# A reordered prefix of an attention and mixture-of-experts block: GpSimd's roots and splits, ScalarE's norms, the first row maxima

## The reference

```
x = x + layernorm(attn(layernorm(x)))
x = x + layernorm(experts(layernorm(x)))
```

```
qq, kq  = Q @ Wc2q + bc2q, K @ Wc2q + bc2q
fid     = (qq . kq) / max(|qq| |kq|, 1e-8)
qw      = fid * (1 + 0.1 sin(pi fid))
probs   = softmax(0.5 qw + 0.5 Q K^T / sqrt(HD))
```

## Time and profile before

| | us |
|---|---|
| median of 3 runs | 478.31 (477.62 to 478.55) |
| the profiled execution | 475.81 |
| its span | 474.1 |

### The profile page before, as it was taken

The page is one execution under the profiler, slowest core; times in us unless marked ns, Lnnn a source line. Parts: engine busy times, 40 slices in busy tenths (PEclk is TensorE's granted clock), DMA queues, the critical chain, the costliest instruction groups (busy, mean ns, idle before and its releaser), DMA issues.

```text
span 474.1 us, 9099 instructions
## 1 busy us (share of the span) xinstructions
PE 369.6 (78%) x2782; PEld 264.2 (56%) x2782; DVE 366.3 (77%) x895; ACT 321.9 (68%) x612; POOL 236.3 (50%) x340
## 2 busy tenths in 40 slices
PE   0976579999999999998998799756010999999950
PEld 0755336666666666665665433635000799999950
DVE  5587798999999999999985533699898148777771
ACT  1347448999999999999877554847510677776620
POOL 7458436555555555555310204000647728887773
PEclk9998858999999999999887999996655799999995
DMA  9606543676666777767719992000103959887400
GB/s 208 23 0 168 125 99 92 149 180 178 170 171 164 169 171 169 170 142 187 164 47 145 148 150 35 1 0 2 42 29 112 271 180 258 242 237 206 108 21 2
DMA packets 87084, 60.87 MB, mean 128 GB/s; under 512 B 16189, under 2 KB 79681, under 8 KB 87030
## 3 DMA queue, kind: packets, MB, share of 16 engines
q1 hardware_dynamic: 79814, 54.69, 52.3%
q0 software_dynamic: 2496, 4.29, 2.6%
q10 hardware_dynamic: 4720, 1.25, 1.3%
HBM read 35.90 MB, written 25.21 MB: 129 GB/s over the span
## 4 chain that ended last, share of the span: by engine, by line
DVE 45%; PE 28%; issue 9%; POOL 8%; ACT 6%; DMA 2%; POOLq 0%; DVEq 0%; SPq 0%; ACTq 0%
DVE big L1841 13%; DVE mxs L1818 11%; DVE big L1871 5%; POOL out_dram L848 5%; PE ps L1623 5%; PE ps L1635 5%; PE ps L1426 3%; PE ps L1211 2%; ACT big L965 2%; PE ps L1525 2%; PE ps L1520 2%; POOL fst L841 1%; DVE gb L1689 1%; DVE u_sb L1880 1%; DVE u_sb L2000 1%
## 5 line engine op out<-in xcount | busy, mean ns | idle before, releaser
L1841 DVE SCALAR_TENSOR_TENSOR big<-big,ps 128x1024 f32<-128x1024 f32 x64 | 74.1, 1215 | 4.2 <-ACT big L955 4.1
L1818 DVE TENSOR_REDUCE mxs<-ps 128x4 f32<-128x1024 f32 x64 | 74.0, 1218 | 1.6 <-PE ps L1248 0.9
L955 ACT ACTIVATE big<-ps 128x1024 f32<-128x1024 f32 x64 | 62.5, 1028 | 7.5 <-PE ps L1391 7.2
L834 POOL DMA_INDIRECT sorted_rows<-proj,sl_i x32 | 33.1, 1036 | 51.4 <-issue 43.6
L848 POOL DMA_INDIRECT out_dram<-arena,fidx x46 | 46.5, 1012 | 15.3 <-issue 9.7
L1623 PE MATMUL ps<-arena,big 128*128 128x256 f32 x184 | 45.3, 390 | 0.6 <-ACT arena L1153 0.6
L1635 PE MATMUL ps<-big,arena 128*128 128x128 f32 x368 | 44.8, 275 | 0.0
L1248 PE MATMUL ps<-arena 96*128 96x256 bf16 x256 | 39.4, 284 | 4.9 <-DVE mxs L1818 2.7
L1635 PEld LDWEIGHTS ps<-big,arena 128*128 128x128 f32 x368 | 42.9, 192 | 0.3 <-ACT arena L1162 0.3
L1871 DVE TENSOR_TENSOR big<-big,ps 128x1024 f32<-128x1024 f32 x32 | 37.9, 1217 | 5.2 <-PE ps L1413 5.1
L753 POOL CAST mtok<-mxs 128x16 bf16<-128x16 f32 x16 | 3.2, 198 | 74.8 <-DVE mxs L1818 74.8
(11 more groups left out here) (347 smaller groups left out, 854.4 us busy)
## 6 DMA issues: line engine op xcount, KB each, us to landing
big<-in_L_ffn_w_dram SPq DMA_DIRECT2D x42, 256.0 KB, 3.3
qk_parts<-proj SPq DMA_DIRECT2D x16, 384.0 KB, 3.2
arena<-qk_parts SPq DMA_DIRECT2D x32, 192.0 KB, 3.5
sorted_rows<-zrow SPq DMA_DIRECT2D x16, 266.0 KB, 5.9
arena<-qk_parts SPq DMA_DIRECT2D x32, 128.0 KB, 4.0
x_all<-sorted_rows SPq DMA_DIRECT2D x23, 133.0 KB, 3.2
sorted_rows<-zrow SPq DMA_DIRECT2D x2, 1263.5 KB, 23.6
sorted_rows<-zrow SPq DMA_DIRECT2D x2, 1197.0 KB, 20.1
```

Source lines behind the costliest of these rows:

```text
L955: nc.scalar.activation(W[par][:, n, :], src, ACT.Sin, scale=PI * (1 - 1e-6)).then_inc(sin_ready, 1)
L1818: nc.vector.tensor_reduce(mxs[:, b1 % 2, :, 2 * n:2 * n + 2], src, AX_X, ALU.max, negate=True).then_inc(unit_free, 1)
L1841: nc.vector.scalar_tensor_tensor(W[par][:, n, :], W[par][:, n, :], 10.0, f, ALU.add, ALU.mult).then_inc(unit_free, 1)
```

## The change

`by_scalar` becomes (2, 4, 5, 6, 7): the norms of groups 5 and 7 move from VectorE to ScalarE, behind the squares of groups 1 and 4. GpSimd takes the root of group 6 ahead of the split of q and k of batch 0, and splits u of batch 0 ahead of q and k of batch 1. All four max units of batch 0 are made before the flag's matmuls or right behind them, three of them ahead of the branch on VectorE; the reciprocals of the second part come between the maxima of batch 1. SyncE's transfers are sorted anew.

```
--- before.py
+++ after.py
@@ -385,7 +385,7 @@
                 return gb[:, 1, :, :].rearrange("p t n -> p (t n)")
             return projf[:, NT * ROW + g * GT * P:NT * ROW + (g + 1) * GT * P]
 
-        by_scalar = (2, 4, 6)
+        by_scalar = (2, 4, 5, 6, 7)
 
 
         SUMS = [("t", 0), ("x", 0), ("t", 1), ("x", 1), ("t", 2), ("t", 3), ("x", 2), ("x", 3)]
@@ -557,15 +557,15 @@
             put_qk(0)
             get_qk(0)
             put_qk(1)
+            put_u(0)
             get_qk(1)
-            put_u(0)
+            get_u(0)
             put_u(1)
-            get_u(0)
             put_qk(2)
+            put_max(0)
             get_u(1)
+            get_max(0)
             get_qk(2)
-            put_max(0)
-            get_max(0)
 
             def body(b, par, first, last, slow):
                 if not last:
@@ -732,12 +732,12 @@
             pool_rstd(4)
             pool_rstd(5)
             ones_under(2)
+            pool_rstd(6)
             split_qk(0)
-            pool_rstd(6)
             pool_rstd(7)
-            split_qk(1)
             root_out(0)
             split_u(0)
+            split_qk(1)
             split_u(1)
             split_qk(2)
             pool.wait_ge(post_loaded, 16 * 17)
@@ -930,10 +930,14 @@
             for g in range(NG):
                 if g + 2 < NG:
                     turn_x(g + 2)
-                if g + 4 < NG and g + 4 in by_scalar:
+                if g in (0, 2):
                     x_norm(g + 4)
                 take_v(g)
                 squares(g)
+                if g == 1:
+                    x_norm(5)
+                if g == 4:
+                    x_norm(7)
                 if g == 2:
                     roots(0)
                     take_qk(2, ps[:, 0, :])
@@ -1336,13 +1340,15 @@
                     turn_u(1)
             pe.wait_ge(qk_out, 3)
             max_unit(0, 0)
+            pe.wait_ge(v_out, NG - 1)
+            max_unit(0, 1)
+            pe.wait_ge(v_out, NG)
+            max_unit(0, 2)
             pe.wait_ge(flag_all, 1)
             for i in range(2):
                 mm = nc.tensor.matmul(ps[0:1, 7, i * P:(i + 1) * P], small[:, 4 + i:5 + i], ident[:, :], start=True, stop=True)
             mm.then_inc(flag_all, 1)
-            pe.wait_ge(v_out, NG)
-            max_unit(0, 1)
-            max_unit(0, 2)
+            max_unit(0, 3)
 
             def body(b, par, first, last, slow):
                 i3 = b % 3
@@ -1439,7 +1445,6 @@
                     mm.then_inc(h_tr, 1)
 
                 if first:
-                    max_unit(0, 3)
                     max_unit(1, 0)
                     turn_max(0)
                     for n in range(1, HP):
@@ -1763,6 +1768,13 @@
                 nc.vector.tensor_scalar(wo_c[:, :], wo_sb[:, :], mean_w[:, 0:1], None, ALU.subtract)
                 nc.vector.tensor_scalar(be2c_bc[:, :], be2_bc, mean_w[:, 1:2], None, ALU.subtract)
 
+            def top(b1, n):
+                dve.wait_ge(unit_ready, unit_no["max", b1, n] + 1)
+                if b1 >= 2:
+                    dve.wait_ge(m_split, 2 * (b1 - 1))
+                src = slot_of("max", b1, n).rearrange("p (h t k) -> p t h k", h=2, t=TPB)
+                nc.vector.tensor_reduce(mxs[:, b1 % 2, :, 2 * n:2 * n + 2], src, AX_X, ALU.max, negate=True).then_inc(unit_free, 1)
+
             ln_stats(0)
             ln_stats(1)
             x_norm(0)
@@ -1804,28 +1816,21 @@
                     clamp(0)
                 if g == 3:
                     reciprocals(0)
+            top(0, 0)
             norm_out(NG - 1)
             root_in(1)
             dve.wait_ge(flag_mins, 2)
             nc.vector.tensor_tensor(small[:, 4:6], small[:, 0:2], small[:, 2:4], ALU.min).then_inc(flag_all, 1)
             clamp(1)
 
-            def top(b1, n):
-                dve.wait_ge(unit_ready, unit_no["max", b1, n] + 1)
-                if b1 >= 2:
-                    dve.wait_ge(m_split, 2 * (b1 - 1))
-                src = slot_of("max", b1, n).rearrange("p (h t k) -> p t h k", h=2, t=TPB)
-                nc.vector.tensor_reduce(mxs[:, b1 % 2, :, 2 * n:2 * n + 2], src, AX_X, ALU.max, negate=True).then_inc(unit_free, 1)
-
-
-            top(0, 0)
+            top(0, 1)
             dve.wait_ge(flag_all, 2)
             nc.vector.tensor_reduce(small[0:1, 6:8], ps[0:1, 7, 0:2 * P].rearrange("p (a n) -> p a n", a=2), AX_X, ALU.min).then_inc(flag_all, 1)
             dve.wait_ge(flag_all, 3)
             nc.vector.tensor_tensor(small[0:1, 0:1], small[0:1, 6:7], small[0:1, 7:8], ALU.mult).then_inc(flag_all, 1)
             dve.wait_ge(flag_all, 4)
             nc.vector.tensor_scalar(flag[0:1, :], small[0:1, 0:1], 1.001 * EPS_COS ** 2, None, ALU.is_lt).then_inc(flag_ready, 1)
-            top(0, 1)
+            top(0, 2)
             before_batches = own_steps[0]
 
             def body(b, par, first, last, slow):
@@ -1881,11 +1886,11 @@
                                             ALU.mult).then_inc(h_done, 1)
 
                 if first:
-                    top(0, 2)
                     top(0, 3)
-                    for n in range(HP):
+                    top(1, 0)
+                    reciprocals(1)
+                    for n in range(1, HP):
                         top(1, n)
-                    reciprocals(1)
                 if slow:
                     norms()
                 if first:
```

25 lines of the change are left out of this document (12 added, 13 removed).

## The result

| | before | after |
|---|---|---|
| median of 7 runs beside each other, us | 477.62 (476.46 to 478.55) | 479.17 (478.71 to 481.62) |
| the profiled execution, us | 475.81 | 478.71 |
| its span, us | 474.1 | 477.0 |

The ratio is 1.0043 with an interval of 1.0023 to 1.0062: by it the changed kernel is about 2 us slower (the two medians differ by 1.55). The forecast was 477.9 and no change, in a range of 476.3 to 479.6. The time lies in the range, but its sign is that of rival 1, the falling clock.

What follows compares the result with a forecast made beforehand. The prediction took batch 0's head as the bound: `make_uv(7)`'s end, then VectorE's path to the third weight. A loss of 0.3, weights 1.2 earlier and a 0.8 stall left -0.4: 477.9 us, range 476.3 to 479.6.

Steps and rivals of the forecast that it cites:

- rival 1: Clock falls in the idle ahead of `make_uv(7)`, which takes 3.48 instead of 1.95: 478.7 to 479.5 us; chance 0.27.
- Norms and root of the early groups: Projections of the prefix: `make_uv(4)` starts at 35.6 instead of 38.55, `make_uv(6)` ends near 45.9, 2.6 us ahead of before.
- The gain is lost at `turn_u(1)`: GpSimd's list holds `turn_u(1)` until 48.6; `make_uv(7)` behind it ends at 50.85 at 2.4 GHz, a loss of 0.3.
- VectorE from `make_uv(7)` on: VectorE's maxima and reciprocals up to batch 0's weights: these could start at 67.0, 1.2 earlier; the branch's 0.77 wait stays.
- the sum: The forecast's total: -0.4 on the profiled execution, 475.81 to 475.4, so a median of 477.9; chance 0.41.
- What is late next: Batch 0's third weight, wanted at 69.3, waits 0.8 for its sine, out at 70.1; the gain left is 0.4.
- The fourth weight: Batch 0's last weight moves from 71.66 to some 72.0, under the transposes and matmuls of unit 0 (3.7 us).
- SyncE at nothing: Batch 1's reads, issued from 50.0 to 52.8 instead of from 44.94, still land before its first max unit: priced at nothing.
- Rival 2: Clock comes back earlier in batch 0, before the transposes: 1.5 us less for transposes and matmuls, 476.4; chance 0.12.
- Rival 3: GpSimd gains when VectorE's norms leave: `turn_u(1)` up to 1.4 earlier, 476.5 us; chance 0.06.
- Rivals 4 and 5: Weights' stall absent, 477.1 us, chance 0.08; or batch 1's reads arrive late, 479.5 us and more, chance 0.06.
- Rival 4: No stall at batch 0's weights, through q and k at 2.4 GHz or a quicker sine: 0.8 more gain, 477.1; chance 0.08.

Runs made afterwards that it cites:

- e12: The kernel before, unchanged, run once more as a kernel of its own: 477.96 us, ratio 0.9999.
- e1: The changed kernel with six matmuls whose output nobody reads, put ahead of `turn_u(1)`: 476.58 us, ratio 0.9990.
- e4: The changed kernel with the old order of maxima, reciprocals and max units: 479.05 us, ratio 1.0051.
- e8: The changed kernel with the reciprocals back behind all four maxima of batch 1: 476.72 us, ratio 1.0008.
- e2: The changed kernel with `turn_u(1)` behind `make_uv(7)` in TensorE's list: 475.96 us, ratio 0.9975.
- e3: The kernel before with only the new order of maxima, max units and reciprocals: 477.40 us, ratio 0.9995.
- e5: e2 with ScalarE's copy of q and k of batch 3 ahead of the third sine, in batch 0 only: 474.97 us, ratio 0.9966.
- e7: e2 with `split_qk(1)` and `get_qk(1)` in their old places and both `turn_u` behind `make_uv(7)`: 474.72 us, ratio 0.9963.
- e11: The changed kernel, unchanged, run once more for a second trace: 479.62 us, ratio 1.0040.
- e6: e2 with fifteen matmuls that nobody reads in four of TensorE's waits: 471.13 us, ratio 0.9887.
- e9: e7 with e5's copy and sixteen filling matmuls, none behind cos unit 2: 474.38 us, ratio 0.9942.
- e10: The kernel before with ten unread matmuls, six ahead of the flag's and four ahead of the branch: 475.49 us, ratio 0.9969.

## Why the prediction was wrong

**Norms and root of the early groups: right.** `make_uv(4)` started at 35.64 (forecast 35.6), at 2.4 GHz (1.97 instead of 3.48). ScalarE normed group 6 from 33.38 (33.4), the copies behind the roots began at 38.12 (38.2), and `make_uv(6)` ended at 45.44 (45.9).

**The gain is lost at `turn_u(1)`: right in place, wrong in price.** GpSimd's `split_u(1)` ended at 48.41 (48.6), and `make_uv(7)` started at 48.70. The failed step is "ends at 50.85 if the clock is 2.4 GHz: a loss of 0.3". It ended at 52.33: a loss of 1.8. This term was priced at the high clock on the strength of one row, the idle of 2.63 ahead of 35.90 at a clock of 1.00. That was a weak precedent. In the same trace the clock fell at 38.2, inside the next idle (of 1.99, up to 38.55), when TensorE had done 0.66 of work since the first one (granted 0.98 from 38.0 to 38.2, 0.50 from 38.2 to 38.4). In e12, the same kernel, it fell at 37.1, also inside that second idle. The idle of the changed kernel was also longer than forecast, 3.02 instead of 2.7; whether 2.7 would have kept the clock no run shows. Rival 1 named this mechanism, its place and a price of at most 1.55; measured were 0.97, 1.31, 1.37 and 1.68 (`make_uv(7)` of 2.92, 3.26, 3.32 and 3.63, less 1.95). It also said that a quarter of `make_uv(7)` at the low clock decides; in the first trace nearly all of it was. It got a chance of 0.27; the clock fell in all four traces with this idle. e1 only fills the idle, and the slowdown goes; e4 has the idle without the new tail, and the slowdown stays. So the step and its place are shown. The one trace that stands across is e8, which has the idle and a `make_uv(7)` of 2.92 at a ratio of 1.0008, with an interval that reaches 1.0037.

**VectorE from `make_uv(7)` on: gain larger than forecast.** Forecast were 67.0 - 50.87 = 16.1 from `take_u(7)` to the weights, measured 15.20. Most of it is the branch: the sum kept its wait of 0.77, but in the changed kernel three maxima around it take 3.63 in one row. The trace of e12 shows 0.30 for it in the kernel before, so the row of 0.77 was one execution's value, not a fixed price.

**What is late next: right, but not complete.** The third weight waited 0.91 for the sine (forecast 0.8; 0.91 to 0.95 in e1, e2, e3, e5, e7 and e11). But the sum ended at the third weight. It followed TensorE's next operands from VectorE only, and left out that `turn_max(1)` and log unit 1 stand ahead of the transposes in TensorE's list, and that `turn_max(1)` waits for ScalarE's `take_qk(3)` behind that same sine. It costs some 0.7. e3 shows both waits without the head: weights 1.5 to 1.7 earlier, transposes level. e5 takes the second away. VectorE's extra gain of 0.9 and this loss nearly cancel (by luck: the sum had neither), so that the clock's term alone, put at 1.8 instead of 0.3, turns the forecast's -0.4 into +1.1, where +0.95 was measured at the transposes.

**The fourth weight: right.** It waited 0.27 and ended at 73.54 (72.32 + 1.22), with TensorE at work on unit 0 until 76.

**SyncE at nothing: right for the changed kernel, since its projections are late.** Nobody waits there for the reads, which were issued from 49.63 to 52.5 (forecast 50.0 to 52.8). In e2, where the projections end 5 us earlier, the same reads cost a wait of 2.07 at the first max unit of batch 1, and e7 gets about 0.8 us back. So the price of nothing held only because TensorE was late.

**Rival 2: not seen.** The granted clock is 0.50 through the transposes and until 76 (the window 66 to 76 above).

**Rival 3: not seen.** With the norms gone `split_qk(0)` still takes 37.00 - 33.29 = 3.71 and `split_qk(1)` 46.37 - 42.65 = 3.72, against 3.72. VectorE in turn shows the wait (start, us, as above):

```profile
31.60 0.17 DVE L1681 COPY mv_all<-mv 128x4 f32<-128x4 f32 x1
...
35.20 0.63 DVE L1681 COPY mv_all<-mv 128x4 f32<-128x4 f32 x1
```

The same small copy takes 0.17, and 0.63 where GpSimd's cast runs from 35.20 to 35.81. This fits the lock that the Trainium skill describes (SBUF — State Buffer, Who interferes with whom), but only VectorE was seen to pay here, and no run was made to test the lock.

**Rivals 4 and 5: not seen.** Rival 4 is what e6 and e9 bring about: with q and k at 2.4 GHz the four weights run in one piece.

**What stays open.** At the transposes the changed kernel is 0.95 late, and at the first heads 0.83; between e11 and e12 it is 0.48 and 0.29. From the first heads to those of the twelfth batch every trace takes the same 131.5 to 131.7. From there to the last heads they take 41.6 to 45.1: 42.8 and 43.4 in the two traces of before, 43.0 and 43.1 in those of the changed kernel, 45.1 in e1. So the last heads of single traces don't tell the kernels apart (267.75 and 267.96 before, 268.70 and 267.95 after, and 268.81 in e1, whose ratio is lower). Nor does a gain at the first heads come through whole: e5 and e7 are 3.3 to 3.8 ahead of before there, and 1.6 to 1.8 by their ratios. The ratios say 1.9 to 2.1 us for the change, and the profiled spans differ by 2.9 and 1.1. What goes beyond the loss at the heads arises in code that the change doesn't touch. Two windows there, of the kernel before and then of the changed one (columns as above):

```profile
270.00:274.00 4.00, 3.45 (x15) 1.17 (x13) 1.46 (x2) 1.69 (x3) 0.80 (x4) 1.00 1.30 135
372.00:377.00 5.00, 4.93 (x30) 4.21 (x29) 0.00 (x0) 3.66 (x10) 3.84 (x4) 0.93 0.89 229
```

```profile
270.00:274.00 4.00, 3.43 (x10) 2.11 (x10) 0.49 (x1) 1.10 (x2) 1.74 (x11) 0.57 1.24 154
372.00:377.00 5.00, 4.94 (x14) 4.04 (x15) 0.00 (x0) 2.52 (x7) 3.78 (x5) 0.56 0.92 239
```

TensorE is as busy in both, but at the low clock it gets through 10 matmuls instead of 15, and 14 instead of 30. The windows don't hold quite the same instructions, since the kernels are shifted by 1 us. They show a difference between these two executions, not between the kernels: e12, the kernel before again, has 0.67 and 0.70 in the same windows. So the part of the 2 us beyond the 0.3 to 0.8 seen at the first heads is not explained. The same holds for the part of e6's and e10's gain that their first heads don't show.

## What to carry to other kernels

When a change moves an engine's work forward but one operand of its next instruction comes from an engine with a full list, what has been won turns into idle time just ahead of that instruction; on TensorE this idle had a price of its own here, 2.92 to 3.63 instead of 1.95 for the eight matmuls behind it. Either move the held instruction behind the work that is ready (e2, 0.9975), or fill the hole (e1, which only takes the slowdown away, 0.9990). And follow the path to the next release through the whole list of the engine that is released, not only through the operand that was last before.
